# Making light attention's first group of 512 rows inside the last steps of the sliding-window layer

## The reference, cut to what matters

```python
def light_attn(x, ln_g, ln_b, w_qkv, w_out):          # on all rows, window 64
    xn = layernorm(x, ln_g, ln_b)
    q, k, v = jnp.split(xn @ w_qkv, 3, axis=-1)       # 8 heads of 64: 512 columns each
    ...                                               # each window attends to itself and both neighbours
def coor_descent(s, k_eff):                           # the router: 50 steps in sequence
    def body(carry, _):
        a, b = carry
        a = logk - logsumexp(s + b); b = -relu(s + a)
```

## Time and profile before

| | us |
|---|---|
| three timed runs | 2637.72, 2653.41, 2658.13 |
| their median | 2653.41 |
| the profiled execution | 2635.35 |
| its span, from the first instruction to the last | 2633.6 |
| PE, DVE, ACT, POOL busy in the span | 87%, 74%, 57%, 51% |
| mean granted clock of PE | 0.924 of full speed |

### The profile page before, as it was taken

How to read it: one execution, slowest core, us unless ns; L and a number is a source line. 1 busy time by engine, 2 the same in 40 slices (tenths; PEclk the granted TensorE clock), 3 DMA queues, 4 the chain that set the end, 5 groups by cost and what they waited for, 6 DMA issues and landing times. The chain is left out here.

```text
span 2633.6 us, 49155 instructions
## 1 busy us (share of the span) xinstructions
PE 2300.1 (87%) x17037; PEld 1610.8 (61%) x17037; DVE 1953.8 (74%) x4315; ACT 1513.2 (57%) x3369; POOL 1331.4 (51%) x1271
## 2 busy tenths in 40 slices
PE   5859898989898997879999978988986999899797
PEld 2545566555656565567777755655653777777555
DVE  5999999999999999256667646777776555566535
ACT  6667778778787875332333324544554666655522
POOL 2787868696868686243323223444565232331411
PEclk7859898999899997989999988999997999898899
DMA  6444443434344444020000134234302000000300
GB/s 199 150 134 149 133 148 128 153 128 153 128 151 136 142 136 132 9 77 1 1 1 1 25 71 77 53 64 69 66 3 75 16 18 22 18 21 15 113 15 9
DMA packets 139463, 206.76 MB, mean 79 GB/s; under 512 B 24481, under 2 KB 59426, under 8 KB 139090
## 3 DMA queue, kind: packets, MB, share of 16 engines
q1 hardware_dynamic: 137234, 200.73, 26.3%
q0 software_dynamic: 960, 2.62, 0.3%
q10 hardware_dynamic: 1024, 0.26, 0.1%
HBM read 161.29 MB, written 14.68 MB: 67 GB/s over the span
## 5 line engine op out<-in xcount | busy, mean ns | idle before, releaser
L427 POOL TENSOR_TENSOR ma_seen<-ma_state,ma_cs 128x1024 f32<-128x1024 f32 x256 | 603.3, 2361 | 265.4 <-DVE ma_state L1069 254.9
L1069 DVE TENSOR_TENSOR_SCAN ma_state<-ma_decay,ma_last,ma_drive 128x512 f32<-128x512 f32 x512 | 650.6, 1271 | 0.0
L1056 DVE TENSOR_TENSOR ma_drive<-ma_weight,ma_bs 128x512 f32<-128x512 f32 x512 | 357.3, 698 | 37.5 <-ACT ma_weight L903 5.6
L647 PEld LDWEIGHTS ma_acc<-ident,ma_seen 128*128 128x128 f32 x2048 | 256.0, 152 | 147.3 <-POOL ma_seen L427 82.2
L647 PE MATMUL ma_acc<-ident,ma_seen 128*128 128x128 f32 x2048 | 290.1, 292 | 57.4 <-POOL ma_seen L427 57.2
L916 ACT ACTIVATE ma_decay<-ma_dt,ma_a_neg 128x512 f32<-128x512 f32 x512 | 338.5, 710 | 0.7 <-DVE ma_dt L1132 0.6
L2197 DVE CUSTOM_DVE_ANT_0 sw_score<-sw_score,both_band 128x256 f32<-128x256 f32 (+1 forms) x512 | 197.3, 447 | 53.1 <-PE sw_score L2011 41.9
L2135 ACT ACTIVATE sw_prob<-sw_turned 128x512 f32<-128x512 f32 (+1 forms) x256 | 135.5, 581 | 175.1 <-PE sw_turned L2025 150.0
L104 POOL TENSOR_TENSOR moe_h_low<-both_V,light_wqkv 128x512 fp32r<-128x512 f32 x80 | 104.8, 1310 | 247.5 <-DVE light_wqkv L100 240.0
L1933 POOL TENSOR_SCALAR_AFFINE_SELECT sw_prob<-sw_prob 128x512 f32<-128x512 f32 x128 | 84.1, 657 | 209.8 <-ACT sw_prob L2135 209.8
L1657 DVE TENSOR_TENSOR both_V<-both_V,moe_up 128x512 f32<-128x512 f32 x80 | 55.0, 687 | 120.6 <-PE moe_up L1446 75.3
(11 more groups left out here) (591 smaller groups left out, 5745.9 us busy)
## 6 DMA issues: line engine op xcount, KB each, us to landing
ma_bs<-bc_rows SPq DMA_DIRECT2D x256, 256.0 KB, 3.3
ma_cs<-bc_rows SPq DMA_DIRECT2D x256, 256.0 KB, 3.2
ma_h<-kept_taps SPq DMA_DIRECT2D x28, 256.0 KB, 4.3
both_wide<-both_kh SPq DMA_DIRECT2D x28, 192.0 KB, 4.5
both_wide<-both_qh SPq DMA_DIRECT2D x20, 256.0 KB, 4.9
x_rows<-X SPq DMA_DIRECT2D x1, 4096.0 KB, 14.2
light_rows<-li_y SPq DMA_DIRECT2D x32, 128.0 KB, 1.7
out_dram<-li_o SPq DMA_DIRECT2D x32, 128.0 KB, 1.8
```

The costliest lines, as they stand in the source:

```text
L427: g.tensor_tensor(out=seen[n % RR][:, :, :], in0=state[n % SR][:, :, :], in1=each(cs[n % CR][:, :], 2), op=ALU.mult).then_inc(S["seen_full ...
L647: ins = t.matmul(accs(j, mm), seen[n % RR][:, mm, j * P:(j + 1) * P], K["ident"][:, :], is_transpose=True, start=False, stop=(last_ and j ...
L1056: v.tensor_tensor(out=drive[mm][:, :], in0=weight[mm][:, :], in1=bs[n % CR][:, :], op=ALU.mult).then_inc(S["drive_done"], 1)
L1069: v.tensor_tensor_scan(state[n % SR][:, mm, :], decay[s % DR][:, :], drive[mm][:, :], last[:, k, m:m + 1], ALU.mult, ALU.add).then_inc(S[" ...
```

## The change

- Sliding steps 22 to 33 get the work of light group 0 but for v. Step 22: `light_stats(r)` on DVE, one tile's mean and variance in each round. Step 23: `light_roots(r)` on POOL. Step 24: `light_row(r)` on ACT, one normed tile in each round. Step 25: two transposed units `lx` (rounds 0 and 2). Steps 26 to 29: one k unit each, `lk`, in round 0; steps 30 to 33: one q unit each, `lq`. All are emptied by ACT (`light_out`). SP loads the gain and bias vectors in the sliding block.
- To keep the results from one block to the next, the keys tensor `light_KT` is allocated first, and the sliding layer's small tensors (`xT`, `qh`, `ql`, `kh`, `kl`, the weights, `band`, `y`, `mq`) and two of the experts' become views of it. The finished k lie where group 0's keys belong, q and xT in columns of later groups (`first_q`, `first_xT`).
- The light opening loses group 0's norms, xT, k and q, group 1's xT, the three weight splits, and four of six router steps. It starts with `scores(0)`; PE makes only the four v units. The selector `pick_head` is no longer made by POOL at full width (one memset, eight selects); POOL makes a seed of 16 columns and ACT copies it out wide, ahead of its first exponentials.
- Group 1 is made a round later (xT in round 0, v ends in round 6). The weight splits and rounds go to the ends of rounds 0 to 2, in the order k, q, v.
- Rounds 0 to 3 do two router steps each: `route_steps`. PE's `total` of the first stands right behind `shifted(R)`, ahead of the units; the second behind `mixes(R-1)`.

```diff
     j, a = (n + 7) // 4, (n + 7) % 4
     if j >= GROUPS:
-        return ()
+        return (((0, "lx", 0, 0), (2, "lx", 0, 1)) if n == 25 else ((0, "lk", 0, n - 26),) if n < 30 else ((0, "lq", 0, n - 30),))
...
+        lxs = [a[:, 1, k * D:(k + 1) * D] for a in (qh, ql) for k in range(2)]
+        lxT = [xT[:, 1, :], kh[:, 1, :]]
+        whole = lambda a: a[:, :, :].rearrange("p h e -> p (h e)")
+        lK = [xT[:, 0, :], ql[:, 0, :], kl[:, 0, :], whole(wv)]
+        lQ = [qh[:, 0, :], kh[:, 0, :], whole(wq), whole(wk)]
...
+            def light_roots(r):
+
+                if r == 0:
+                    pool.wait_ge(S["lmv_done"], GT)
+                    g.tensor_scalar(lmv[:, :, 1], lmv[:, :, 1], 1.0, LN_EPS, ALU.mult, ALU.add).then_inc(S["lroot_in"], 1)
+                if r == 1:
+                    g.tensor_scalar(lshift[:, :], lmv[:, :, 0], -1.0, 0.0, ALU.mult, ALU.add).then_inc(S["lroot_in"], 1)
+                if r == 2:
+                    pool.wait_ge(S["lroot_in"], 2)
+                    g.tensor_tensor(out=lrstd[:, :], in0=lmv[:, :, 1], in1=K["neghalf"][:, :], op=ALU.pow).then_inc(S["lrstd_done"], 1)
+                if r == 3:
+                    pool.wait_ge(S["lrstd_done"], 1)
+                    g.tensor_tensor(out=lshift[:, :], in0=lshift[:, :], in1=lrstd[:, :], op=ALU.mult).then_inc(S["lshift_done"], 1)
...
+                elif kind == "lx":
+                    pe.wait_ge(S["lxs_full"], GT)
+                    for a in range(GT):
+                        ins = t.transpose(out[:, a * P:(a + 1) * P], lxs[a][:, m * P:(m + 1) * P], K["ident"][:, :])
+                elif kind in ("lk", "lq"):
+                    pe.wait_ge(S["wqkv_in"], 16)
+                    pe.wait_ge(S["lx_full"], DH)
+                    at = (HW if kind == "lk" else 0) + m * P
+                    for hh in range(DH):
+                        ins = t.matmul(out[:, :], K["wqkv"][:, hh, at:at + P], lxT[hh], start=(hh == 0), stop=(hh == DH - 1))
...
+            def light_row(a):
+
+                if a == 0:
+                    act.wait_ge(S["lshift_done"], 1)
+                    for into in q_in:
+                        came(act, into, 3 * (GROUPS - 1))
+                a_.activation(lxs[a], xc(a), ACT.Identity, scale=lrstd[:, a:a + 1], bias=lshift[:, a:a + 1]).then_inc(S["lxs_full"], 1)
+
+            def light_out(kind, m):
+                out = filled(kind, 0, m)
+                if (kind, m) == ("lx", 0):
+                    act.wait_ge(S["thin_in"], 32)
+                    act.wait_ge(S["v_full"], GT * (GROUPS - 1))
+                    for into in k_in + k_last_in:
+                        came(act, into, 3 * (GROUPS - 1))
+                if kind == "lx":
+                    a_.activation(lxT[m], out[:, :], ACT.Identity, scale=K["gain"][:, m:m + 1], bias=K["bias"][:, m:m + 1]).then_inc(S["lx_full"], 1)
+                if kind == "lk":
+                    act.wait_ge(S["lx_full"], DH)
+                    a_.activation(lK[m], out[:, :], ACT.Copy).then_inc(S["lk_full"], 1)
+                if kind == "lq":
+                    act.wait_ge(S["k_low"], DH * (GROUPS - 1))
+                    a_.activation(lQ[m], out[:, :], ACT.Copy, scale=DHD ** -0.5).then_inc(S["lq_full"], 1)
...
+                    if n == 24:
+                        light_row(r)
...
+            def light_stats(a):
+
+                dve.wait_ge(S["x_done"], a + 1)
+                v.bn_stats(lstat[:, a, :], xc(a)).then_inc(S["lstat_done"], 1)
+                dve.wait_ge(S["lstat_done"], a + 1)
+                v.bn_aggr(lmv[:, a, :], lstat[:, a, :]).then_inc(S["lmv_done"], 1)
...
+                    if n == 22:
+                        light_stats(r)
...
+COLUMNS = (1, 0, 2)
+AT_FIRST = 2
+
+
+def route_steps(R):
+
+
+    if R >= OPENING - AT_FIRST:
+        return [R + OPENING]
+    return [AT_FIRST + 2 * R, AT_FIRST + 2 * R + 1]
...
-        at = R - (8 * (j - 1) - 1)
+        at = R - (8 * (j - 1) - (0 if j == 1 else 1))
...
+            made.chain(g.memset(seed[:, :, :], 0.0))
             for at in range(2):
                 for k in range(PARTS):
-                    made.chain(g.affine_select(out=pick_head[:, :, :], in_=pick_head[:, :, :], compare_op=ALU.not_equal, fill=1.0,
-                                               base=-(WIN * at + LH * k), pattern=[[-1, LH], [0, P]], channel_multiplier=1))
+                    made.chain(g.affine_select(out=seed[:, :, :], in_=seed[:, :, :], compare_op=ALU.not_equal, fill=1.0,
+                                               base=-(WIN * at + LH * k), pattern=[[-1, LH], [0, 2]], channel_multiplier=1))
             for at in range(2):
                 up = slice(WIN * at + 32, WIN * at + WIN)
-                made.chain(g.affine_select(out=pick_head[up, :, :], in_=pick_head[up, :, :], compare_op=ALU.not_equal, fill=1.0, base=0,
-                                           pattern=[[0, LH], [-1, 2], [0, WIN]], channel_multiplier=1))
+                ins = g.affine_select(out=seed[up, :, :], in_=seed[up, :, :], compare_op=ALU.not_equal, fill=1.0, base=0,
+                                      pattern=[[0, LH], [-1, 2]], channel_multiplier=1)
+                if at == 0:
+                    made.chain(ins)
+            ins.then_inc(S["seeded"], 1)
+            pool.wait_ge(S["seeded"], 1)
...
+            scores(0)
             pe.wait_ge(S["max_done"], 1)
             t.transpose(tops, part[:, :], K["ident"][:, :]).then_inc(S["max_turned"], 1)
+            ahead("v", 0, 0)
             pe.wait_ge(S["max_diag"], 1)
             pe.wait_ge(S["made"], made_steps[0])
             t.matmul(small, ones[0:PROBLEMS, :], diag[:, :], start=True, stop=True).then_inc(S["max_spread"], 1)
-            for m in range(DH):
-                ahead("xT", 0, m)
-            for kind, first_ in (("k", 0), ("q", 2)):
-                for half in range(2):
-                    for m in (2 * half, 2 * half + 1):
-                        ahead(kind, 0, m)
-                    total(first_ + half)
-            for R_ in range(2):
-                scores(R_)
-                ahead("v", 0, 2 * R_)
-                ahead("v", 0, 2 * R_ + 1)
-                total(4 + R_)
-            for unit in light_ahead(-1):
-                ahead(*unit)
+            ahead("v", 0, 1)
+            scores(1)
+            total(0)
+            ahead("v", 0, 2)
             scores(2)
+            ahead("v", 0, 3)
             pe.wait_ge(S["made"], made_steps[1])
             turn(0)
+            total(1)
             scores(3)
-            pe.wait_ge(S["w_in"], LOADED)
-            pe.wait_ge(S["made"], made_steps[2])
+            pe.wait_ge(S["picked"], 1)
             for R_ in range(HALVES + 2):
                 n, r = divmod(R_, 2)
                 units = light_ahead(R_)
                 if R_ < HALVES:
                     shifted(R_)
+                for i in route_steps(R_)[:-1]:
+                    total(i)
+                if R_ == 1:
+                    pe.wait_ge(S["w_in"], LOADED)
                 for unit in units[0:1]:
                     ahead(*unit)
+                if R_ == FIRST_DIGIT:
+                    pe.wait_ge(S["made"], made_steps[2])
                 if FIRST_DIGIT <= R_ < FLAGS:
                     tallies(2 * (R_ - FIRST_DIGIT))
...
+                if len(route_steps(R_)) > 1:
+                    total(route_steps(R_)[1])
...
+            act.wait_ge(S["seeded"], 1)
+            a_.activation(pick_head[:, :, :].rearrange("p h (a q) -> p (h a) q", q=WIN), over(seed[:, :, :].rearrange("p h a -> p (h a)"), WIN),
+                          ACT.Copy).then_inc(S["picked"], 1)
+            query_exps(0)
             route_exp(0)
-            for i in range(2):
-                route_log(i)
-                route_exp(i + 1)
-            for half in range(2):
-                copies("q", 0, 2 * half)
-                copies("q", 0, 2 * half + 1)
-                route_log(2 + half)
-                weights_round(half)
-                route_exp(3 + half)
-            query_exps(0)
-            route_log(4)
-            route_exp(5)
             query_exps(1)
-            route_log(5)
-            weights_round(2)
             logs(0)
-            for unit in light_ahead(-1):
-                copies(*unit)
+            route_log(0)
+            route_exp(1)
+            query_exps(2)
             shift_rows(0)
-            query_exps(2)
+            route_log(1)
...
+                for i in route_steps(R_)[:-1]:
+                    route_log(i)
+                for unit in units[0:1]:
+                    copies(*unit)
+                for i in route_steps(R_)[1:]:
+                    route_exp(i)
+                for unit in units[1:]:
                     copies(*unit)
                 if R_ == HALVES:
                     unit_out(0)
...
+                if R_ < PARTS:
+                    weights_round(R_)
...
             v.tensor_reduce(part[:, :], s[:, :, :], AXX, ALU.max).then_inc(S["max_done"], 1)
```

(48 more changed lines are left out.)

148 lines of the change are left out of this document (79 added, 69 removed).

## The result

The changed kernel is slower, by less than half a percent. Over 21 executions of each its median is 2650.84 us (2641.81 to 2658.83) against 2639.67 (2628.28 to 2658.13) of the kernel before; the ratio is 1.0036, with a 95% interval of 1.0021 to 1.005, so +5.5 to +13 us. Over all 82 executions of the kernel before the mean is 2647.6 us, against 2650.6 of the changed one. So the sign and the size of the total are weaker than the interval says, and what follows rests on the stretches. The profiled execution has a span of 2640.1 us (before 2633.6), at a mean granted clock of 0.926 (0.924).

What follows compares the result with a forecast made beforehand. It took PE and DVE handing over scores to bound sliding steps, a chain the opening, PE the rounds. 11.0 - 30.0 + 15.0 + 5 + 1.6 = +2.6 us on 2646 gave 2649 us, range 2628 to 2668.

Steps and rivals of the forecast that it cites:

- The sliding steps: Sliding steps 22 to 33: new units and statistics partly absorbed in PE's gaps; +11.0 us, from 5 to 20.
- at nothing: Steps 26 to 29: ACT's 512-column copies lie beside PE's work, costing nothing; about 0.6 us each if that cover goes.
- term for step 25: Two transposes, 0.66 us each: the first fits PE's gap, the second costs 0 to 0.66; taken as 0.4 us.
- The opening: Light stage start to scores(3): shorter chain, beginning with ACT's wait for POOL's seed; -30.0 us, from -32 to -26.
- Rounds 0 to 3: Two router steps per round, PE waiting some 3 us for the first total; +15.0 us (+7 to +20), plus +5 for PE's clock.
- Rounds 4 to 7: Round 6 gets a pair of units and loses a 1.15 us wait, +1.6 us; from round 7 nothing differs.
- The rule weighed in the prediction: Opening: two-SBUF-input VectorE and GpSimd operations exclude each other; would delay DVE, which has slack, and not the chain.
- (b): Rival, rounds 0 to 3: the double rounds are nearly hidden; -15 us, 2631 us; chance 0.20.
- (c): Rival, sliding steps: `turn` waits for ACT's copy of each unit, nothing absorbed; net +19, 2665 us; chance 0.10.
- three signs of a wrong forecast: Sliding-step PE waits on ACT's copies; rounds 0 to 3 under 35 us; opening over 30 us with ACT waiting for POOL.
- (d): Rival: PE stays at 1.2 GHz through rounds 0 to 3, +16 instead of +5; net +14, 2660 us; chance 0.10.
- (e): Rival, opening: not shortened as planned, such as seed selects of 1.2 us each holding ACT; net +10; chance 0.05.

Runs made afterwards that it cites:

- other tiles: Changed kernel with the second turned row tile written over the k weights, two tiles taking other memory; median 2647.33 us, 0.9986 of the kernel before.
- half units: Kernel whose turned rows take other memory, each sliding k and q unit one product instead of two, results differ; 2643.84 us, one execution.
- four steps out: Changed kernel without four of the router's fifty iterations, one step per round, results differ; median 2634.06 us, 0.992 of the kernel before.
- filled wait: Changed kernel with eight useless PE products where PE waits for the first router total; 2638.99 us, one execution, rounds 0 to 3 45.06 us.
- spread steps: Changed kernel with both router steps of rounds 0 to 3 kept but reordered on PE, ACT and DVE; median 2644.81 us, 0.9979 of the kernel before.
- total behind the units: Changed kernel with PE's first router total moved behind the projection units in rounds 0 to 3; median 2640.35 us, 0.9962 of the kernel before.

## Why the prediction was wrong

The forecast of +2.6 us was too low by about 11 in the stretches (+13.8), and by 3 to 11 by the timed ratio. That 2649 lies near the measured 2650.84 shows nothing: it was made on a base of 2646, and the kernel before came out at 2639.67 over 21 executions. By the terms:

**The sliding steps, +11.0 forecast, +21.1 measured: the step that failed.** The working puts ACT's copies in these steps "at nothing", and its term for step 25, 0.4 us, counts PE's two transposes alone. It missed that ACT waits for `k_in` and `k_last_in` ahead of the first of the two copies, since the second one overwrites `kh`, a tile that those placements read. In step 25 the last of them are still on their way, since they are issued only behind `shifted` of step 24. The rule stated at the outset, what is queued behind a waiting instruction and who waits for that, was applied to the rounds and not here. The kernel with other tiles shows its price: 9.6 us, 6.9 of it the wait with what follows in step 25 and 2.7 the low clock in step 26. The rest is +11.5 and was near the forecast of 11.0, though not in each part. Steps 27 to 29 cost +1.0 each (forecast 1.14), steps 30 and 31 +1.23 and +1.26 (1.39), 32 +1.10 (1.25), the end +0.9 (0.8), and half units confirms how the gap takes its part. The transposes of step 25 cost nothing (0.4). Steps 22 to 24 cost 3.1 where 1.2 was counted. Of this, 2.6 are in steps 22 and 23, where DVE has the four statistics and PE waits longer for its maxima, first before, then after:

```profile
1867.60 0.33 PE L2007 MATMUL sw_score<-both_wide,both_QP 48*128 48x128 f32 x2 [0.93 <-DVE sw_most L2197]
```

```profile
1864.37 0.33 PE L2052 MATMUL sw_score<-both_wide,both_QP 48*128 48x128 f32 x2 [1.51 <-DVE sw_most L2270]
```

The mean granted clock of the two steps is 0.90 after and 0.95 before. They take 31.1 us before, and 33.3 to 33.8 in all eleven traces that have the change; there is one trace of before, so whether the change also brings the lower clock isn't shown.

**The opening, -30.0 forecast, -29.6 measured: right.** The seed came at +5.3 (4.5, range 3.7 to 5.2), the scores at +23.9 (23.5). What the forecast had seen, ACT's wait for POOL with all exponentials behind it, was worth 4.3 us to remove.

**Rounds 0 to 3, +15.0 and +5 for the clock, +21.4 measured: right in size and in kind.** 17.6 us go with the four second steps by the kernel with four steps out, the clock's part among them; filled wait has 4.3 for the clock. The two overlap and don't add up to the 21.4. By rounds it was 9.4, 13.8, 13.0, 13.1 against 9.3, 10.4, 11.2, 12.0 without the clock: round 1 is the one that was most under-counted. A part of its 3.4 us is DVE's weight split: counted as 1.9 us, it took 3.8 beside POOL in the changed kernel.

```profile
2030.42 1.63 DVE L100 TENSOR_SCALAR li_V<-light_wqkv 128x1024 uint32<-128x1024 uint32 x1
...
2032.08 2.18 DVE L104 TENSOR_TENSOR heavy_wqkv<-light_wqkv,li_V 128x1024 fp32r<-128x1024 f32 x1
```

The waits on PE are 2.6, 3.6, 2.3 and 3.4 us where "some 3" were forecast.

**Rounds 4 to 7, +1.6 forecast, +0.9 measured.**

**The rule weighed in the prediction.** It was expected to hold up DVE in the opening, where DVE has slack, and so to change nothing. It bit in round 0 instead. The rows of the kernel with four steps out first: DVE's L100 1.48 instead of 0.43 us, its L104 2.18 instead of 1.23, POOL's `x_low` running each time. The Trainium skill, SBUF — State Buffer, "SBUF: two separate sides", calls the pair of ports that VectorE and GpSimd share an exclusive lock for the whole instruction, not a split of bandwidth; the trace agrees: a DVE instruction is late by what is left of POOL's, and POOL's second `x_low` (1.78 us, the first took 1.26) by what was left of DVE's.

**The rivals.** (b), rounds nearly hidden, fell: the order written in the change doesn't hide them, though the kernel with spread steps gets 11.4 of the 21.4 back. (c) named the place, `turn` behind ACT's copy of a unit, and one of the three signs of a wrong forecast, "a PE wait in the sliding steps on ACT's copies", is there at 3.48 us. But it happens in one step, by a DMA, not in each by the copies' length, and costs 9.6 us and not 19. (d), PE at 1.2 GHz through the rounds, is true of the clock in most of rounds 0 and 1 (0.55 and 0.56) and half of round 2 (0.74), and wrong in its price: it doubled PE's work, +16, where most of that lies beside the chain anyway; a clock of 0.92 in place of 0.69 gave 4.3. (e) fell: six seed selects took 2.15 us.

## What to carry to other kernels

When work is moved to an earlier place, list the waits that its tiles bring along, not only its durations: reusing a buffer whose last reader is a DMA puts that DMA into the queue of the engine that writes it, and everything behind it there pays. A wait belongs behind all work of that engine that doesn't need it; one line moved on PE gave back 9 us here, and a copy moved on ACT 4. A term for PE's clock is worth having, but it is to be taken against the chain beside it, not as PE's work doubled.

## What the hardware showed beyond that

Whether PE's granted clock falls isn't settled by what PE did just before. Step 31 of the sliding block has the same code and the same waits in the kernel after and in that with other tiles. It took 9.09 us at a clock of 1.00 in the one and 10.66 at 0.84 in the other, where the fall came at 1977.13, one microsecond into the step, and ran through the dense work behind it:

```profile
1974.66 1.98 PE L2023 MATMUL sw_bank<-light_KT,light_wqkv 128*128 128x512 f32 x4
```

```profile
1978.62 2.92 PE L2023 MATMUL sw_bank<-light_KT,light_wqkv 128*128 128x512 f32 x4
```

Ahead of the fall PE had waited 1.08 us for ACT, until 1974.88; the kernel after has the same wait, until 1971.55. Here are the 5 us up to the fall, then the same stretch of the kernel after, where none came. On PE they are alike to a hundredth:

```profile
1972.13:1977.13 5.00, 3.81 (x56) 2.68 (x55) 1.39 (x5) 2.85 (x7) 2.23 (x5) 1.00 0.02 5
```

```profile
1968.80:1973.80 5.00, 3.81 (x56) 2.68 (x55) 1.39 (x5) 2.86 (x7) 2.23 (x5) 1.00 0.02 5
```

Steps 22 and 23 are like this. The kernel after has them at 17.41 and 16.31 us, both at 0.90; the kernel with the total behind the units, whose code is that of after there, at 18.72 and 14.65, at 0.82 and 1.00: another place and, within 0.4 us, the same sum. Such falls cost some 1.6 us each, come in some executions and not in others, and were seen in steps all over the sliding block, also far ahead of the change (14.44 us at 1.00 against 16.14 at 0.89 for the third one). In the twelve traces each fall from the third sliding step on comes shortly behind waits of PE, such as the 1.51 us one in step 22 or this one of 1.08. The Trainium skill, TensorE: Matmul & The Clock Gate, "Part 1: The HAM clock gate", has the throttled clock as the default that activity releases; these rows agree in so far as every fall there follows waits. What decides between a fall and none behind the same waits stays open. These falls are a part of why executions of one kernel lie 20 us apart. Before a difference of 1.6 us in a step is put down to an edit, its clock has to be compared.
